# A conditioned transformer block: q and k turned by DMA transposes, V sent through DRAM

## The reference, cut to what matters

```python
qkv = (x @ qkv_w + qkv_b).reshape(n, t, 3, H, DH)        # H 16, DH 18
q, k, v = qkv[:, :, 0], qkv[:, :, 1], qkv[:, :, 2]
attn = softmax(einsum('nthd,ntkd->nthk', q * scale, k))  # 16 x 16 per token
out = einsum('nthk,ntkd->nthd', attn, v)
```

## Time and profile before

| | |
|---|---|
| median of 3 runs | 427.33 us (426.06 to 427.52) |
| span of the profiled execution | 422.3 us; its own time is not listed apart from the span |
| TensorE busy | 397.1 us, 94% of the span |
| VectorE busy | 291.1 us, 69% |
| ScalarE busy | 231.8 us, 55% |
| GpSimd busy | 115.9 us, 27% |
| DMA | 7926 packets, 14.68 MB, mean 35 GB/s; q1 busy for 11.0% of 16 engines' span |
| chain that ended last | TensorE 71%, VectorE 14%, ScalarE 10%, issue 4% |
| qkv loop | 121 to 217.6 us |
| attention loop | 217.6 to 281.5 us |

### The profile page before, as it was taken

How to read it: one execution, slowest core, us unless ns; L and a number is a source line. 1 busy time by engine, 2 the same in 40 slices (tenths; PEclk the granted TensorE clock), 3 DMA queues, 4 the chain that set the end, 5 groups by cost and what they waited for, 6 DMA issues and landing times.

```text
span 422.3 us, 11278 instructions
## 1 busy us (share of the span) xinstructions
PE 397.1 (94%) x4547; PEld 256.5 (61%) x4547; DVE 291.1 (69%) x793; ACT 231.8 (55%) x485; POOL 115.9 (27%) x137
## 2 busy tenths in 40 slices
PE   8999999999989899899978898889999999999996
PEld 4656555666545566666646565558755566666675
DVE  2688875677689856667757766666899776746452
ACT  3356334433257899997786785665775342422100
POOL 5039999981008700000000000005420010101040
PEclk9999989999989999999999999999999999999999
DMA  6999000000000000000000000000000000000011
GB/s 166 305 316 271 24 4 2 12 7 2 2 0 2 2 2 3 2 2 5 2 4 3 5 4 4 4 2 2 0 2 1 16 28 16 23 20 16 29 43 42
DMA packets 7926, 14.68 MB, mean 35 GB/s; under 512 B 2555, under 2 KB 6239, under 8 KB 7748
## 3 DMA queue, kind: packets, MB, share of 16 engines
q1 hardware_dynamic: 7874, 13.96, 11.0%
HBM read 11.52 MB, written 2.38 MB: 33 GB/s over the span
## 4 chain that ended last, share of the span: by engine, by line
PE 71%; DVE 14%; ACT 10%; issue 4%; ACTq 0%; DVEq 0%
PE psum L957 13%; PE psum L973 13%; PE psum L517 9%; PE psum L803 6%; ACT scratch L1068 3%; PE psum L787 2%; PE psum L880 2%; PE psum L617 2%; DVE MX L1373 2%; ACT big L1101 2%; PE psum L934 2%; PE psum L629 2%; PE psum L751 2%; PE psum L573 2%; PE psum L608 2%
## 5 line engine op out<-in xcount | busy, mean ns | idle before, releaser
L957 PE MATMUL psum<-scratch,W 128*128 128x512 f16 (+1 forms) x252 | 57.9, 379 | 0.0
L973 PE MATMUL psum<-W,big 128*128 128x288 f16 x432 | 55.1, 286 | 0.0
L506 POOL TENSOR_TENSOR X<-X,big 128x288 f32<-128x288 f32 x16 | 13.0, 826 | 150.0 <-ACT big L1174 149.7
L803 PE MATMUL psum<-WQ,scratch 128*128 128x288 f16 (+1 forms) x336 | 50.5, 294 | 2.8 <-DVE scratch L1368 1.9
L1199 ACT ACTIVATE big<-psum 128x512 f32<-128x512 f32 x36 | 21.3, 597 | 57.3 <-PE psum L957 52.3
L973 PEld LDWEIGHTS psum<-W,big 128*128 128x128 f16 x432 | 42.2, 98 | 12.9
L1373 DVE TENSOR_REDUCE MX<-psum 128x8 f32<-128x1024 f32 x32 | 39.0, 1220 | 11.4 <-PE psum L751 11.0
L517 PE MATMUL psum<-ident 128*32 128x192 f32 (+3 forms) x142 | 43.8, 393 | 0.0
L1129 ACT ACTIVATE big<-psum 128x1024 f32<-128x1024 f32 x32 | 32.9, 1032 | 15.0 <-PE psum L843 14.7
L957 PEld LDWEIGHTS psum<-scratch,W 128*128 128x128 f16 (+1 forms) x252 | 24.6, 98 | 25.6
L803 PEld LDWEIGHTS psum<-WQ,scratch 128*128 128x128 f16 (+1 forms) x336 | 30.6, 100 | 14.8 <-DVE scratch L1368 2.4
(11 more groups left out here) (221 smaller groups left out, 770.5 us busy)
## 6 DMA issues: line engine op xcount, KB each, us to landing
X<-in_x_dram SPq DMA_DIRECT2D x4, 576.0 KB, 14.8
out_dram<-big SPq DMA_DIRECT2D x16, 144.0 KB, 1.7
big<-in_L_cond_W_dram SPq DMA_DIRECT2D x1, 2268.0 KB
big<-in_L_cond_ada_w_dram SPq DMA_DIRECT2D x2, 864.0 KB, 18.2
stage<-in_L_cond_fc_w_dram SPq DMA_DIRECT2D x1, 1296.0 KB, 18.9
big<-in_L_cond_fc_w_dram SPq DMA_DIRECT2D x1, 1152.0 KB
stage<-in_L_cond_qkv_w_dram SPq DMA_DIRECT2D x1, 864.0 KB
big<-in_L_cond_fc_w_dram SPq DMA_DIRECT2D x3, 144.0 KB
```

Of the source, the lines that this page charges most:

```text
L803: mm = pe.matmul(UB[gu % 2][:, 0:D], HT[0:r, n % 2, a_, P * a:P * a + P], WQ[0:r, w_, D * w:D * w + D], start=(p_ == 0), stop=(p_ == 6))
L957: mm = pe.matmul(FB[idx % 3], W1[0:r, w_, P * m:P * m + P], HT[0:r, n % 2, a_, :], start=(p_ == 0), stop=(p_ == 6))
L973: mm = pe.matmul(YB[t % 2][:, 0:D], g[:, a_, f, cols], W2[:, w_, f, :], start=(f == 0 and a_ + w_ == 0), stop=(f == NF - 1 and w_ == 1))
```

## The change

The 64-column parts of q and k of two tiles now lie side by side in HQ ([2 pairs, q or k, head, tile of the pair, 64]), so that 128 f16 columns are one head of both tiles. For each pair and each of q and k, SP issues one DMA transpose of 128 partitions by 2048 f16 columns, from HQ to QKT (`turn_heads`). QKT's columns are then in order of head and token, and `operand` reads them with a stride; the permuted identity `order` goes, and `turn` uses `ident`.

V is no longer split. `high` copies its f32 result to one of four buffers SV, `store_values` sends it to DRAM (`value_rows`), and `spread_values` brings one pair's rows back in eight DMAs of 16 partitions by 32 rows by 18 f32, straight to its slots in VG. VG has six buffers instead of two; GpSimd clears them and sets their ones instead of VectorE. `max_turn` goes: ScalarE scales MX as it is (128x64 f16) and four DMAs per chunk, of 128 partitions by 16 f16, write the row. All jobs, `v_late`, `v_groups` and their copies go. The qkv loop has three PSUM banks instead of two. ScalarE's write of HQ for pair `pr` waits for the transposes of pair `pr - 2`. The core of the diff:

```diff
-        SELV = sb("SELV", [P, DH], F16)
-        ident16 = sb("ident16", [P, P], F16)
...
-        MRT = sb("MRT", [64, NCH, P], F16)
+        MRT = sb("MRT", [P, 2, 64], F16)
...
-        VG = scratch[:, 0:4 * CH].rearrange("p (a c g d) -> p a c g d", a=2, c=2, g=16)
+        VGS = [big[:, 8192 + 2 * CH * i:8192 + 2 * CH * (i + 1)] for i in range(4)] + [scratch[:, 2 * CH * i:2 * CH * (i + 1)] for i in range(2)]
+        VG = [v.rearrange("p (c g d) -> p c g d", c=2, g=16) for v in VGS]
...
-        HQ = stage[:, 0:4096].bitcast(F16).rearrange("p (a w h c) -> p a w h c", a=TPC, w=2, h=H)
+        SV = scratch[:, o:o + 4 * D].rearrange("p (a d) -> p a d", a=4)
+        assert o + 4 * D <= 4 * 2112 + 2 * D
+        HQ = stage[:, 0:4096].bitcast(F16).rearrange("p (a w h e c) -> p a w h e c", a=2, w=2, h=H, e=2)
...
-        UB, CB = [bank[2], bank[5]], [bank[6], bank[7]]
+        UB = [bank[2], bank[5], bank[6]]
...
-            return QKT[b][R * c_:R * c_ + rows, w, P * (4 * u + g):P * (4 * u + g + 1)]
...
+            pr, v = divmod(4 * u + g, 16)
+            cols = QKT[b][R * c_:R * c_ + rows, w, 16 * P * pr:16 * P * (pr + 1)]
+            return cols.rearrange("p (t v) -> p v t", v=16)[:, v]
...
+            def store_values(pr, c_):
+                k = 2 * pr + c_
+                sp.wait_ge(v_copied, k + 1)
+                sp.dma_start(values_d[pr, :, c_], SV[:, k % 4, :]).then_inc(v_stored[k % 4], 16)
+
+            def turn_heads(pr, w):
+                if pr == NCH and w == 0:
+                    sp.wait_ge(x_rot, NT)
+                    sp.wait_ge(folded, 2 * B)
+                sp.wait_ge(qk_low, lows(6 * pr + 3 + w))
+                dst = QKT[pr // NCH][:, w, 16 * P * (pr % NCH):16 * P * (pr % NCH + 1)]
+                sp.dma_start_transpose(dst.rearrange("p (h t) -> p h t", h=H),
+                                       HQ[:, pr % 2, w].rearrange("p h e c -> p (h e c)")).then_inc(qk_in[pr], 16)
+
+            def spread_values(w):
+                for c_ in range(2):
+                    sp.wait_ge(v_stored[(2 * w + c_) % 4], 16 * (w // 2 + 1))
+                if w < 6:
+                    sp.wait_ge(vg_clear, 2 if w < 4 else 4)
+                else:
+                    sp.wait_ge(pv_ready, 4 * (w - 6) + 4)
+                for m in range(8):
+                    src = bass.AP(tensor=values_d.tensor, offset=values_d.offset + (2 * P * w + 32 * m) * D, ap=[[DH, H], [D, 32], [1, DH]])
+                    sp.dma_start(VGS[w % 6].rearrange("p (g d) -> p g d", d=32)[m:P:8, :, 0:DH], src).then_inc(v_in[w], 16)
...
             def max_row(n):
-                if n < 2:
-                    sp.wait_ge(col_done, JOB[("max", n)] + 1)
-                else:
-                    sp.wait_ge(mr_ready, n - 1)
+                sp.wait_ge(mr_ready, n + 1)
                 for c_ in range(2):
-                    at = 32 * P * (n % 2)
-                    row = QKT[n // 2][R * c_ + MROWS:R * c_ + MROWS + 1, 0, at:at + 32 * P]
-                    sp.dma_start(row.rearrange("p (u j) -> p u j", u=32), MRT[32 * c_:32 * c_ + 32, n, :]).then_inc(max_in[n], 16)
-
-            for n in range(NCH):
+                    for k in range(2):
+                        at = 16 * P * (2 * (n % 2) + k)
+                        row = QKT[n // 2][R * c_ + MROWS:R * c_ + MROWS + 1, 0, at:at + 16 * P]
+                        sp.dma_start(row, MRT[:, n % 2, 32 * c_ + 16 * k:32 * c_ + 16 * k + 16]).then_inc(max_in[n], 16)
+
+            for pr in range(2 * NCH):
+                store_values(pr, 0)
+                turn_heads(pr, 0)
+                turn_heads(pr, 1)
+                store_values(pr, 1)
+                if 1 <= pr < 5:
+                    spread_values(pr - 1)
+                if pr == 6:
+                    max_row(0)
+            spread_values(4)
+            spread_values(5)
+            for n in range(1, 3):
                 max_row(n)
+                spread_values(5 + n)
+            max_row(3)
...
             for a_ in range(2):
                 pool.memset(HT[96:P, a_, 4, :], FINE).then_inc(ht_ones, 1)
                 pool.wait_ge(ht_ones, a_ + 1)
+            pool.wait_ge(fill_done, FG + 1)
+            pool.memset(big[:, 8192:12288], 0.0).then_inc(vg_clear, 1)
+            pool.wait_ge(vg_clear, 1)
+            pool.memset(big[:, 8192:12288].rearrange("p (g d) -> p g d", d=32)[:, :, DH:DH + 1], 1.0).then_inc(vg_clear, 1)
+            pool.wait_ge(vg_clear, 2)
...
+            pool.memset(scratch[:, 0:4 * CH], 0.0).then_inc(vg_clear, 1)
+            pool.wait_ge(vg_clear, 3)
+            pool.memset(scratch[:, 0:4 * CH].rearrange("p (g d) -> p g d", d=32)[:, :, DH:DH + 1], 1.0).then_inc(vg_clear, 1)
...
-                        if n < NCH:
-                            mm = pe.transpose(f[0:rows, cols], XN[:, n % 2, j, r0:r0 + rows], order[:, :])
-                            continue
...
-                    pe.wait_ge(col_done, JOB[(s_ // 4, 1, 3)] + 1)
+                    pe.wait_ge(qk_in[s_ // 4], 32)
...
-                if gu >= 2:
-                    pe.wait_ge(qk_low, gu - 1)
+                if gu >= 3 and w == 2:
+                    pe.wait_ge(v_copied, gu // 3)
+                elif gu >= 3:
+                    pe.wait_ge(qk_low, lows(gu - 3))
...
-                    pe.wait_ge(max_in[s_ // 8], 32)
+                    pe.wait_ge(max_in[s_ // 8], 64)
...
-                    pe.wait_ge(mr_ready, 2)
+                    pe.wait_ge(mx_used, UNITS)
...
-                    pe.wait_ge(vg_ready, w + 1)
+                    pe.wait_ge(v_in[w], 128)
...
-            pe.wait_ge(col_done, JOB[(NCH - 1, 2, 3)] + 1)
...
-            pe.wait_ge(col_done, len(jobs))
-            v_groups(0)
+            pe.wait_ge(qk_low, lows(NQ * NCH - 1))
+            pe.wait_ge(v_copied, NT)
...
+                pr, e = 2 * n + i // 2, i % 2
                 act.wait_ge(qk_ready, gu + 1)
+                if w == 2:
+                    k = gu // 3
+                    if k >= 4:
+                        act.wait_ge(v_stored[k % 4], 16 * (k // 4))
+                    act.mul(SV[:, k % 4, :], UB[gu % 3][:, 0:D], 1.0 / (FINE * FINE)).then_inc(v_copied, 1)
+                    return
                 if gu == 0:
-                    act.wait_ge(att_const, 1)
...
+                    act.wait_ge(att_const, TPC)
+                if pr >= 2:
+                    act.wait_ge(qk_in[pr - 2], 32)
+                src = UB[gu % 3][:, 0:D].rearrange("p (h d) -> p h d", h=H)
+                dst = HQ[:, pr % 2, w, :, e, 0:HALVES].rearrange("p h (s d) -> p h s d", s=3)
                 act.mul(dst[:, :, 0:2, :] if w else dst[:, :, 0:3:2, :], src.unsqueeze(2).broadcast_to([P, H, 2, DH]),
                         QSCALE / (FINE * FINE)).then_inc(qk_high, 1)
 
...
+            def rows_out(n):
+                act.wait_ge(mx_used, 8 * (n + 1))
+                if n >= 2:
+                    act.wait_ge(max_in[n - 2], 64)
+                act.mul(MRT[:, n % 2, :], MX[:, n, :], 1.0 / MROW).then_inc(mr_ready, 1)
...
+            act.wait_ge(folded, 2 * B)
...
                 if w == 2:
-                    hi, lo = HV[:, 4 * (n % 2) + i, :, 0, :], HV[:, 4 * (n % 2) + i, :, 1, :]
...
-                dve.scalar_tensor_tensor(out=lo, in0=src, scalar=QSCALE / (FINE * FINE), in1=hi,
+                    return
...
                     dve.wait_ge(weights, 5)
+                    for pr in range(2 * NCH):
+                        dve.wait_ge(qk_in[pr], 32)
```

More of the change, by code:

```diff
@@ L297, in build @@
         MROWS = HALVES + 8
[L298 to L307, removed]
         AHEAD = {24 + 3 * s_ // 2: s_ for s_ in range(16)}
         LATER = {st: 1 for st in range(16)}
-        ROWS_LATER, ROWS_BANK = {8: 2, 16: 3}, {8: VB[0], 16: MXB[0]}
+        ROWS_EARLY = {36: 0, 3 * 4 * NCH: 1}
+        ROWS_LATER = {8: 2, 16: 3}
         PAIRED = 18
@@ L433, in _ @@
                     chain(pool.tensor_copy(II[R * g:R * g + R, R * h:R * h + R], ident[R * g:R * g + R, R * g:R * g + R]))
-            chain(pool.tensor_copy(order.rearrange("p (v m) -> p v m", v=16), ident.rearrange("p (m v) -> p v m", m=8)))
             pool.memset(MOD[:, :, :, :], 0.0).then_inc(consts, 1)
@@ L441, in _ @@
                                      pattern=[[0, 1]], channel_multiplier=1))
-            chain(pool.tensor_copy(SELV[:, :], ident[:, 0:DH]))
-            for j in (DH, R, R + DH):
-                chain(pool.tensor_tensor(SELV[:, :], SELV[:, :], ident[:, j:j + DH], ALU.add))
             for src, dst, n, s_ in ((SWQ, WQ, 3 * D, in_wq), (SW1, W1, MLP, in_w1)):
@@ L822, in _ @@
                     qkv(gu)
-                for i in slots.get(gu, ()):
-                    job(i)
                 if gu in AHEAD:
@@ L910, in _ @@
                     values(st - 1)
-                if st in ROWS_LATER:
-                    pe.wait_ge(vg_ready, st // 4 + 1)
-                    max_turn(ROWS_BANK[st], ROWS_LATER[st]).then_inc(mr_psum, 1)
```

(13 more changed lines are left out.)

167 lines of the change are left out of this document (33 added, 134 removed).

## The result

The changed kernel takes 456.77 us in the median of its runs against 427.29 before; the ratio is 1.066 [1.062, 1.071]. It is slower by 6.6%, where 5.5% faster was forecast, and outside the range. The profiled run is the first, with a span of 451.1.

What follows compares the result with a forecast made beforehand. TensorE and ScalarE were taken as full in the qkv loop because of the jobs, attention as paced by a chain. 26.1 + 10.1 - 11.6 - 1 = 23.6 us off 422.3 gave 398.7, plus 5.0: 404 us, range 388 to 424.

Steps and rivals of the forecast that it cites:

- What the loops lose: Qkv and attention loops: removed jobs, groups and copies take off 26.1 us and 10.1 us.
- rival (a): Maxima and scores operands: strides are free, with 3 us for the queue; 33.2 us off, 394 us; chance 0.28.
- strided operands: Maxima and scores matmuls: reads 32 bytes apart cost 0.21 us per group of eight, 11.6 us in sum.
- Rival (d): Maxima and scores operands: strides cost four times, not twice; another 23 us, 427 us, no change; chance 0.04.
- The clock: Stretches where TensorE idles more: a granted clock of 0.50 was named as a possible cost, not counted.
- the DMA queue: SP's queue: transposes at 2.4 us and spreads at 4.5 are covered by compute; 1 us counted.
- Rival (b): SP's queue sets the loop's pace, by slower transposes and spreads or spreads alone; 414 or 420 us; chance 0.17.
- (c): Transposes on SP's queue: written piece by piece, 6.9 us each, they throttle ScalarE's `high`; 456 us; chance 0.11.

Runs made afterwards that it cites:

- a_contig: The changed kernel with maxima and scores operands read as 128 neighbouring columns instead of one column in every 16: 419.5 us, 0.985 of before.
- c_nospread: The changed kernel with operands of neighbouring columns and without the 64 DMAs that bring V to its slots: 398.3 us, 0.933 of before.
- b_strided: The kernel before, with only the operands of maxima and scores read with one column in every 16: 474.2 us, 1.113 of before.
- c_onedma: The changed kernel with neighbouring columns, V of a pair brought by one DMA instead of eight, stores in small pieces too: 425 us, 0.997 of before.

## Why the prediction was wrong, step by step

- **What the loops lose**: right in kind. No L787, L764 or L866 group is left. With neither cost (and without V's way back) the kernel takes 398.3 us, where rival (a), the same sum without strides and with 3 us for the queue, said 394. Its qkv loop ends at 200, not at the 192 to 195 of my terms.
- **The failed step, strided operands**: "I take the upper, 0.21 us per group of eight, on the assumption that a read which uses 2 bytes of every 32 is not free; half speed is the first step below free that the rows show." The direction was right, the size was not: 0.75 us per group (1.15 for 0.40), and 36 to 47 us in all, half clock included, where I had 11.6. The "upper" end was no bound. It was a row of neighbouring reads at another clock, taken because it was there; no row of before says how slow a strided read can be, and the range should have said so. Rival (d), "strides cost four times", was the right mechanism near the right price (0.84 us a group) and had 0.04. That its 11.6 + 23 = 35 us are the 36 measured beside the spreads is in part luck, as those hold the half clock, which (d) left out.
- **The clock**, a term put at nothing: "A clock of 0.50 in stretches where TensorE now idles more would be a cost that I have not counted." It came, and in stretches where TensorE doesn't idle at all. Values and turns are busy 47.0 us in the change and 32.3 in `a_contig`.
- **The failed step, the DMA queue**: "I count 1 us", because everything was "covered". Alone it costs 21 us, in the change 15. What was too short is the time that a DMA holds SP. A transpose held it for 2.8 us in the median where I had 2.4; without spreads about it was 2.0 to 2.3, so my figure was one of an undisturbed queue. A spread took 5.3 to 6.2 for 4.5. The landing of transposes was right: 4.8 us from the start, 2 after the end. So a turn of the queue was 13.2 us where my terms make 10.1, and a pair's six units take 9.9 in `c_nospread` (79 us for eight pairs). By my own terms a turn with a spread was already longer than a pair of the forecast loop, 70.5 / 8 = 8.8; I had looked only at two points of the sum, each covered by 2 to 4 us. `max_row(1)` leaves at 228 where my sum had it landed at 208. Rival (b) had this mechanism and nearly its size (414 to 420 against 419.5 without strides). It stood at 0.17 because I let two lengths a fifth too short add up to a cover.
- **Transposes written piece by piece** (c): its time, 456, is the one measured, by another cause. It needs transposes of 6.9 us each on the queue, and they held it for 2.8. A forecast that had named (c) would have been right by accident.
- **The chances**: both costs were among the rivals, each by itself. The case in which both hold had no line of its own, and it is the one that came: 398 for neither, 21 for the queue and 36 for the strides beside it, 456.

## What to carry to other kernels

A layout that saves copies by letting matmuls read with a stride is paid at every read: look at the moving operand first, count the 16-byte pieces that its columns touch, and measure one such group before building on it. A DMA queue that serves several consumers needs its turn compared with the loop's turn, by the time that each DMA holds the queue when the others stand beside it; fewer DMAs with the same pieces didn't shorten the turn here. When a change has several parts, time each alone: here V by DRAM gains 3.4% and q and k by transposes, with strided reads, lose more than that.

## What the runs showed of the hardware

- Eight matmuls of 128 f16 columns take 0.40 us at full clock with columns 2 or 4 bytes apart, 0.64 at 8 bytes, 1.13 at 16 and 1.16 at 32; the mean duration of one is 231, 227, 291, 414 and 423 ns. It is the moving operand that pays: 1.09 us a group with it alone at 32 bytes, 0.46 with the stationary one alone. The Trainium skill, "SBUF — State Buffer", Door 1, says that lines are 16 bytes, that two hits per line are needed, and that bf16 may stride 8 elements for free. The runs, with f16, agree on the lines. They don't on the 8 elements: at 8 the full price is paid, at 4, with two hits, a third of it, and only at 2 none.
- A group at 32 bytes takes as long at a granted clock of 0.50 as at 1.00 (1.16 and 1.15 us in the change, 1.16 and 1.16 in `b_strided`, where no DMA runs); only its neighbours slow down (values 1.08 us for 0.64).
- The granted clock fell to 0.50, that is 1.2 GHz, in stretches in which TensorE was busy without a gap and two of every three groups were strided, with DMAs (share 0.59) and without (0.01). The kernel before had shown 0.95 or more in each part of its loops.
- A DMA transpose of 128 x 2048 f16 within the state buffer holds SP for 2.0 to 2.3 us in the median with no spreads about, and for 2.5 to 3.1 in the kernels that spread V by the order of the change. It lands 4.6 to 4.9 us after its start in the median of each kernel, and 5.5 in `c_onedma`.
